# A two-attention, two-FFN sandwich on one core: one routing pass ahead of the scatters, and ScalarE applying the norms around the second attention's first tiles

## The reference

```python
x = x + LN(attn0(LN(x)))   # 16 heads of 64; x is 2 x 1024 x 128, float32
x = x + LN(ffn0(LN(x)))    # shared MLP, plus 8 experts with top-2 routing
x = x + LN(attn1(LN(x)))   # differential attention, 8 heads of 2 x 128
x = x + LN(ffn1(LN(x)))    # gated MLP with two hidden layers

def ffn0(h):
    n = h * rsqrt(mean(h*h) + 1e-8) * norm_weight
    shared = relu(n @ sw1 + sb1) @ sw2 + sb2
    probs = sigmoid(n @ router_w.T)              # 8 experts
    scores, idx = top_k(probs, 2)
    w = scores / (sum(scores) + 1e-6)
    return shared + sum_k w[k] * expert[idx[k]](n)
```

## Time and profile before

| | |
|---|---|
| three runs | 1982.66, 1984.46, 1985.24 us; median 1984.46 |
| profiled execution | 1987.63 us, with a span of 1985.6 us between the first and last instruction |
| busy in the span | PE 1826.1, DVE 1556.2, ACT 1354.5, POOL 1196.3 us |
| granted TensorE clock, mean | 0.972 of full |

### The profile page before, as it was taken

The page is one execution under the profiler, slowest core; times in us unless marked ns, Lnnn a source line. Parts: engine busy times, 40 slices in busy tenths (PEclk is TensorE's granted clock), DMA queues, the critical chain, the costliest instruction groups (busy, mean ns, idle before and its releaser), DMA issues.

```text
span 1985.6 us, 36444 instructions
## 1 busy us (share of the span) xinstructions
PE 1826.1 (92%) x11162; PEld 1557.8 (78%) x11162; DVE 1556.2 (78%) x2682; ACT 1354.5 (68%) x2739; POOL 1196.3 (60%) x1473
## 2 busy tenths in 40 slices
PE   4969999999999999976886899999999999999787
PEld 3858888878888888865775688888888888888666
DVE  5958999989989998964477877777777777777774
ACT  3848888878888887832454577777777777777555
POOL 4535655554656555653554677777777777777621
PEclk9989999999999999987998899999999999999899
DMA  2292121212121213021210000000000000100000
GB/s 71 47 86 50 45 48 45 50 46 48 45 50 45 48 45 94 22 86 55 67 57 30 4 1 12 1 11 0 11 0 11 0 11 0 66 1 1 1 11 11
DMA packets 68531, 65.95 MB, mean 33 GB/s; under 512 B 27712, under 2 KB 47040, under 8 KB 68128
## 3 DMA queue, kind: packets, MB, share of 16 engines
q1 hardware_dynamic: 65888, 59.02, 13.3%
q0 software_dynamic: 2496, 5.15, 0.7%
HBM read 21.33 MB, written 9.25 MB: 15 GB/s over the span
## 4 chain that ended last, share of the span: by engine, by line
PE 77%; DVE 9%; issue 5%; ACT 4%; SPq 2%; POOL 2%; DMA 1%; another core or an unknown queue 1%; DVEq 0%; ACTq 0%; POOLq 0%
PE ps_t L625 7%; PE ps_o L635 6%; PE ps_s L657 5%; PE ps_s L658 5%; PE ps_o L636 5%; PE ps_s L1831 5%; PE ps_s L1829 5%; PE ps_s L1830 5%; PE ps_t L1887 3%; PE ps_o L1903 3%; PE ps_o L1905 3%; PE ps_o L1904 3%; PE ps_t L1323 2%; DVE a_negmax L2033 1%; PE ps_m L614 1%
## 5 line engine op out<-in xcount | busy, mean ns | idle before, releaser
L807 DVE TENSOR_REDUCE a_negmax<-ps_s 128x1 f32<-128x1024 f32 x256 | 313.3, 1224 | 70.7 <-PE ps_s L658 57.2
L2033 DVE TENSOR_REDUCE a_negmax<-ps_s 128x1 f32<-128x1024 f32 x256 | 312.5, 1221 | 67.5 <-PE ps_s L1831 64.8
L738 ACT ACTIVATE a_pth<-ps_t 128x512 fp32r<-128x512 f32 x512 | 279.4, 603 | 115.4 <-PE ps_t L625 115.3
L1961 ACT ACTIVATE a_p<-ps_s,a_negmax 128x1024 f32<-128x1024 f32 x256 | 286.8, 1120 | 95.6 <-DVE a_negmax L2033 94.6
L793 DVE TENSOR_TENSOR a_ptl<-ps_t,a_pth 128x512 fp32r<-128x512 f32 x512 | 327.8, 682 | 6.5 <-ACT a_pth L738 6.2
L873 POOL TENSOR_TENSOR a_rsum<-a_sum,minus_one 128x1 f32<-128x1 f32 x256 | 141.1, 551 | 312.7 <-ACT a_p L768 310.1
L877 POOL TENSOR_SCALAR a_p<-a_p,a_rsum 128x1024 f32<-128x1024 f32 x256 | 289.8, 1132 | 53.4 <-POOL a_rsum L873 53.4
L2131 POOL TENSOR_TENSOR a_p<-a_p 128x1024 f32<-128x1024 f32 x128 | 307.5, 2402 | 10.7
L768 ACT ACTIVATE a_p<-ps_s,a_negmax 128x1024 f32<-128x1024 f32 x256 | 289.2, 1130 | 13.8 <-DVE a_negmax L807 13.8
L657 PE MATMUL ps_s<-a_kh,a_q 128*128 128x512 f32 x512 | 202.8, 396 | 30.5 <-DMA a_kh<-a_kh 26.9
L635 PE MATMUL ps_o<-a_pth,a_v 128*128 128x512 f32 x512 | 220.8, 431 | 7.2 <-DVE a_ptl L793 4.5
(11 more groups left out here) (299 smaller groups left out, 4155.7 us busy)
## 6 DMA issues: line engine op xcount, KB each, us to landing
a_q<-a_kh SPq DMA_DIRECT2D x64, 128.0 KB, 2.2
a_q<-a_kl SPq DMA_DIRECT2D x64, 128.0 KB, 2.4
a_kh<-a_kh SPq DMA_DIRECT2D x64, 128.0 KB, 2.2
a_kl<-a_kl SPq DMA_DIRECT2D x64, 128.0 KB, 2.3
a_w_raw<-in_l_w SPq DMA_DIRECT2D x8, 384.0 KB
f_xs_rows<-f_zero SPq DMA_DIRECT2D x4, 736.0 KB, 17.3
f_raw<-in_ffn_w SPq DMA_DIRECT2D x2, 1408.0 KB, 8.1
f_xs<-f_xs_rows SPq DMA_DIRECT2D x2, 1235.0 KB, 7.3
```

Of the source, the lines that this page charges most:

```text
L807: dve.tensor_reduce(a0_negmax[:, s % 4:s % 4 + 1], ps_s[:, s % 2, :, :], AX.XY, ALU.max, negate=True)\
L2033: dve.tensor_reduce(a1_negmax[:, s % 2, m:m + 1], ps_s[:, m, :, :], AX.XY, ALU.max, negate=True)\
```

## The change

It has two parts.

Part one, the head of the first FFN. The low parts of the FFN's first weights move from POOL to DVE (`f0_pool_w1_lo` becomes `f0_dve_w1_lo`, one ahead of the routing, four and four between `shared` steps). All four chunks are normed, turned and given logits first; then one routing pass handles all 16 tiles (`f0_dve_route(dve)`, operands twice as long), one `f0_pe_prefix` both groups, and only `f0_dve_place` stays per group. PE's shared MLP comes behind all logits. `f0_left` and `f0_tmp2` are gone; `f0_taken` and `f0_sum` have a group dimension. Chunk 3 turns through a bank of `ps_s`. On DVE the last `pt_lo` of the attention comes ahead of a norm.

Part two, the norms around the second attention's first tiles, chunks 0 to 3. `x1_apply` moves from DVE to ACT as an activation with a scale and a bias; POOL's `norm_factors` also makes that bias, -mean x rstd. The sum into X stays on DVE (`x1_sum`). In the first head the table becomes `X1_DVE`: both halves of the combination come a slot or more earlier, and chunk 3's norm ends in slot 5 and not in slot 7. POOL's factors stand ahead of its scaling and summing in slots 2 to 5, and the keys of chunks 2 and 3 come in slots 5 and 7 instead of 6 and 9.

```diff
@@ a0_dve, after the last slot
             pt_lo(g - 2, SLOTS - 2)
-            y0_norm(dve, 4, 0)
-            pt_lo(g - 1, SLOTS - 1)
             dve.wait_ge(S["a0_out_added"], n - 2)
             y0_norm(dve, 0, 1)
-            add_out(n - 2, 2)
+            pt_lo(g - 1, SLOTS - 1)
+            y0_norm(dve, 4, 0)
+            dve.wait_ge(S["a0_pv"], 4 * H0 - 1)
             for stage in range(1, 4):
                 y0_norm(dve, stage, 1)
-            f0_dve_turn(dve, 0)
+            add_out(n - 2, 2)
@@ f0_pe
-            up(0)
             f0_pe_turn(pe, 1)
             pe.wait_ge(S["a0_out_added"], 2 * H0)
             f0_pe_logits(pe, 0)
             f0_pe_logits(pe, 1)
-            down(0, lambda: route(0))
-            up(1)
-            down(1)
             f0_pe_turn(pe, 2)
-            up(2)
-            pe.wait_ge(S["f0_prefix_out"], 1)
             f0_pe_logits(pe, 2)
-            down(2)
             f0_pe_turn(pe, 3)
             f0_pe_logits(pe, 3)
-            up(3)
-            down(3, lambda: route(1))
+            up(0)
+            down(0, lambda: f0_pe_prefix(pe))
+            for c in range(1, NC):
+                up(c)
+                down(c)
@@ f0_dve
+            for stage in (1, 2, 3):
+                y0_norm(dve, stage, 2)
+            f0_dve_turn(dve, 0)
+            for stage in (1, 2, 3):
+                y0_norm(dve, stage, 3)
+            y0_norm(dve, 4, 2)
+            f0_dve_turn(dve, 1)
+            y0_norm(dve, 4, 3)
...
+            f0_dve_w1_lo(dve, 0)
+            f0_dve_route(dve)
             f0_dve_place(dve, 0)
...
+            f0_dve_turn(dve, 2)
+            f0_dve_turn(dve, 3)
             shared(0)
-            f0_dve_turn(dve, 2)
+            f0_dve_place(dve, 1)
+            for pos in range(1, 5):
+                f0_dve_w1_lo(dve, pos)
             shared(1)
-            y0_norm(dve, 4, 3)
-            f0_dve_turn(dve, 3)
+            for pos in range(5, NE):
+                f0_dve_w1_lo(dve, pos)
             shared(2)
-            f0_dve_route(dve, 1)
-            f0_dve_place(dve, 1)
-            expert = f0_read_words(dve)
-            shared(3)
             for g in range(NG):
                 f0_dve_weights(dve, g)
+            shared(3)
+            expert = f0_read_words(dve)
@@ norm_factors, new
+        def norm_factors(pool, n, par):
+            mean = mv[:, par, :, 0]
+            pool.wait_ge(S["norm_var"], n + 1)
...
+            pool.tensor_scalar(mean, mean, -1.0, 0.0, ALU.mult, ALU.add)
+            pool_rsqrt(pool, rstd[:, par, :], mv[:, par, :, 1], EPS_LN).then_inc(S["pool_step"], 1)
+            pool.wait_ge(S["pool_step"], pool_steps.next())
+            pool.tensor_tensor(mean, mean, rstd[:, par, :], ALU.mult).then_inc(S["norm_rstd"], 1)
@@ x1_apply, x1_sum
-        def x1_apply(dve, c, i):
+        def x1_apply(act, c, i):
+            par = x1_par(c, i)
+            act.wait_ge(S["norm_rstd"], NORM_F0 + 2 * c + i + 1)
+            act.wait_ge(S["x1_summed"], from0(c - 1 + i))
+            for k in range(TPC):
+                t = c * TPC + k
+                ins = act.activation(tile(Y, t) if i else tile(xhat, k), tile(X if i else Y, t), ACT.Identity,
+                                     scale=rstd[:, par, k:k + 1], bias=mv[:, par, k, 0:1])
+            ins.then_inc(S["x1_ready" if i else "x1_applied"], 1)
+        def x1_sum(dve, c):
+            dve.wait_ge(S["x1_applied"], c + 1)
+            xc = X[:, c * TPC:(c + 1) * TPC, :]
+            dve.tensor_tensor(xc, xc, xhat[:, :, :], ALU.add).then_inc(S["x1_summed"], 1)
@@ the first head's slots
-        X1_SLOTS = {1: ((x1_combine, 2, 0), (x1_combine, 2, 1)), 2: ((x1_stats, 2, 0),), 3: ((x1_apply, 2, 0), (x1_stats, 2, 1)),
-                    4: ((x1_apply, 2, 1), (x1_combine, 3, 0), (x1_combine, 3, 1)), 5: ((x1_stats, 3, 0),),
-                    6: ((x1_apply, 3, 0), (x1_stats, 3, 1)), 7: ((x1_apply, 3, 1),)}
+        X1_DVE = {1: (("combine", 2, 0), ("combine", 2, 1)), 2: (("stats", 2, 0), ("combine", 3, 0)),
+                  3: (("sum", 2), ("stats", 2, 1)), 4: (("combine", 3, 1), ("stats", 3, 0)), 5: (("sum", 3), ("stats", 3, 1))}
+        X1_FACTORS = {2: (2, 0), 3: (2, 1), 4: (3, 0), 5: (3, 1)}
```

More of the change, by code:

```diff
@@ L173, in sandwich_kernel @@
         f0_to = sb("f0_to", [P, NB])
-        f0_taken = sb("f0_taken", [P, GT + 3, NR])
-        f0_sum = [sb(f"f0_sum{i}", [P, GT + 5, NR]) for i in range(2)]
+        f0_taken = sb("f0_taken", [P, NG, GT + 3, NR])
+        f0_sum = [sb(f"f0_sum{i}", [P, NG, GT + 5, NR]) for i in range(2)]
         f0_rows = sb("f0_rows", [P, GT + 1, NR])
@@ new lines, in f0_dve_route @@
+            first, second = (f0_one[:, k, :, :].rearrange("p (g t) e -> p g t e", g=NG) for k in range(2))
+            a, b = f0_sum
+            step(dve.tensor_tensor(f0_taken[:, :, 2:GT + 2, :], first, second, ALU.add))
+            step(dve.tensor_tensor(a[:, :, 4:, :], f0_taken[:, :, 1:GT + 2, :], f0_taken[:, :, 0:GT + 1, :], ALU.add))
+            step(dve.tensor_tensor(b[:, :, 4:, :], a[:, :, 4:, :], a[:, :, 2:GT + 3, :], ALU.add))
+            dve.tensor_tensor(a[:, :, 4:, :], b[:, :, 4:, :], b[:, :, 0:GT + 1, :], ALU.add)\
@@ L1386, in block_relu @@
                 ins.then_inc(S["f0_b_relued"], 1)
-            f0_act_turn(act, 1)
-            f0_act_probs(act, 0)
-            relu(0)
-            relu(1)
-            f0_act_turn(act, 2)
-            relu(2)
-            f0_act_turn(act, 3)
-            f0_act_probs(act, 1)
-            relu(3)
+            for c in range(1, NC):
+                f0_act_turn(act, c)
+            f0_act_probs(act)
+            for c in range(NC):
+                relu(c)
             expert = f0_read_words(act)
@@ L1719, in a1_act_prepare @@
                 a1_act_q(act, i + 1, (0, *Q_PIECES[i]), ps_m[:, :])
+            if n in A1_APPLY:
+                x1_apply(act, *A1_APPLY[n])
         def a1_dve_prepare(dve, n):
@@ L2019, in slot @@
                     softmax(g, s, 1)
+                if first and s in X1_FACTORS:
+                    x1_apply(act, *X1_FACTORS[s])
                 if last and SLOTS - 4 <= s < SLOTS + 2:
@@ L2091, in slot @@
                     negmax(g, s, 0)
-                    if first and s in X1_SLOTS:
-                        for work, c, i in X1_SLOTS[s]:
-                            work(dve, c, i)
+                    if first and s in X1_DVE:
+                        x1_dve(dve, s)
                     spare_lo(h, s, first, last)
@@ L2149, in slot @@
                     rms(h, s)
+                if first and s in X1_FACTORS:
+                    c, i = X1_FACTORS[s]
+                    norm_factors(pool, NORM_F0 + 2 * c + i, x1_par(c, i))
                 if s == M_SLOT and not first:
```

140 lines of the change are left out of this document (54 added, 86 removed).

## The result

| | before | changed |
|---|---|---|
| runs | 1982.66 to 1985.84 us, median 1984.85 | 1970.04 to 1970.78 us, median 1970.49 |
| ratio of the two | | 0.9929, 95% interval 0.9917 to 0.9942 |
| profiled execution, span | 1987.63, 1985.6 us | 1970.77, 1968.2 us |
| granted TensorE clock, mean | 0.972 | 0.976 |

A forecast was written before the change was run, and what follows sets the result against it. Only PE's waits at the attention's end, first FFN's head and second attention's first head could give time; head 2, loop 1, first head 14 make 17 us: 1967.5 from the median, own range 1961 to 1975, 8-in-10 range 1949 to 1980.

The forecast's parts named there:

- head, with the hold: First FFN's head: if signals are held behind the scatters, first block at 922.4 against 923.97; 2 us gained.
- block loop: FFN block loop: four norm applications leave DVE for ACT, which is not the busiest; 1 us gained, -1 to 3.
- first head: Second attention's first head: PE's waits for chunks 2 and 3 shrink; 14 us gained, bounds 8 to 16.
- The range's own lower terms: Lowest gains in the forecast's own range: head 0, loop -1, first head 8 us; given as 1975.
- The hold recurs: First FFN's head: the run of 16 scatters holds `relu(2)` until 901.9, 1.8 us behind its end; first block 922.4.
- Rival, no hold: First FFN's head: PE ends the shared MLP inside the scatter run; head gains 16.5, total 31.5 us, 1953; chance 0.30.
- The three waits: First head: PE's waits of 9.72, 4.62 and 4.37 us fall by 5.2, 4.6 and 4.4, in all 14.2.
- the sum `L1800`: First head: DVE's sum of two SBUF inputs may be blocked beside POOL; takes 0.69 or 3.1 us.
- Rival, slower: First head, slots 2 to 5: POOL's factors ahead of scaling and summing delay PE, 4.5 us a slot; 1990; chance 0.06.

The follow-up runs named there:

- p1_head: The kernel before with only the first part of the diff (the first FFN's head), norms as before; ratio to before 0.9994 (0.9983 to 1.0005).
- second and third group: Follow-up kernels timed beside the kernel before on chips 11 and 8; the kernel before took 1964.7 and 1968.0 us there.
- l_late: The changed kernel with ACT's norms in the block loop, their sums and second statistics one block later; 1946.8 us (one run).
- h_pace: The changed kernel with a small POOL power operation behind each pair of the first group's scatters; 1967.26 us (one run).

## Why the prediction was right, and where it was not

The time, 1970.49, lies in the range and 3 us from the forecast 1967.5. The terms did less well than their sum, so part of that closeness is luck: the head gave more in the profile, the loop and the first head less.

| term | forecast | measured |
|---|---|---|
| head, with the hold | 2 | 6.7 in the profile, 4.0 in that of `p1_head`, 1.2 (-1.0 to 3.4) by the runs of `p1_head` |
| block loop | 1 | -2.0 in the profile; 0.4 where nothing is held |
| first head | 14 | 11.1, and 11.9 without the hold |

The range's own lower terms (0, -1 and 8) add to 7 us, which is 1977.5 and not the 1975 given; the outcome does not hang on it.

**The hold recurs.** Right, in place, and in its end (2.2 us behind the last scatter, 1.8 forecast). Wrong in what it catches: forecast was that `relu(2)` stops dead; it was stretched by 0.7 to 1.4 us a piece, and the stop came one chunk later. With `relu(2)` done, only `relu(3)` and `down(3)` stood behind the release: 12.1 us from there to the first block, where the forecast had 20.5. The release itself came 3.0 us later (904.90, not 901.9), so the first block is 5.4 us earlier than forecast, and with a low clock in `down(3)` (6.58 us in `p1_head`) 2.7 of it go again.

**Rival, no hold.** Its mechanism was seen in full in the second and third group, at a first block of 909.09 where the forecast said 907.5. Its gain of 16.5 us in the head was not: the kernel before loses its hold as well (A + B 84.5), and the difference is 8.0. The forecast compared the changed kernel without a hold to the old one with it.

**Loop.** The step said that ACT's four norms lie in its slack, with a gain of 1. The term is mis-sized: without the hold the gain is 0.4. ACT's time did lie in its slack (1.65 us each, 1.15 by the nearest row), but its wait did not: the order of ACT's list puts `block_relu` behind a wait for POOL's factors, and the prediction did not name what is queued behind that wait. That this ate what DVE's relief gave is likely and not shown; `l_late`, with the wait gone, takes 5 us out of the loop. With the hold the loop lost 2.0, 1.5 of them ahead of ACT's first norm; why is not known.

**First head.** The three waits were foreseen as 14.2 us less. Those for the turns fell by 6.5 and 4.2, as forecast 5.2 and 4.4; the third fell by 3.0 of 4.6. New waits of 0.98 (for POOL's `a_p`) and 1.25 us came in, both from POOL's lateness. The Trainium skill ("SBUF — State Buffer", section "SBUF: two separate sides") has VectorE's operations with two SBUF inputs shut out beside GpSimd operations that read SBUF. The trace agrees: where I had looked for it, at the sum `L1800`, it cost 1.1 us once; where I had not, at a one-column `a_c` with two SBUF inputs, it cost 2.1 us twice.

**Rival, slower.** Its mechanism, factors ahead of scaling and summing, is real: 4.7 us over four slots, 1.2 a slot, where 3.5 would have turned the sign.

What stays open: by which way a run of indirect DMAs holds PE's signals, and why in one group and not in the others. Each group ran on another chip and at another time, and no kernel was timed on two chips in one group or on one chip in two, so the chip and the moment can't be told apart.

## What to carry to other kernels

Work that moves to an engine with slack brings its waits with it: look at what is queued behind the wait, and place the work one step after its input is sure to be there; here that was worth 5 us, while taking the work off DVE had gained 0.4 in that stretch. Do the same for the producer: a small reciprocal root ahead of a long pass on POOL made every later tile late. And a gain that rests on a stall should be priced against a kernel before that may not have the stall either.

## What was not expected of the hardware

An unbroken run of POOL's indirect DMAs (of 5 to 16, one every 1.27 us) delayed PE's signals to ACT and DVE, first by 0.7 to 1.4 us each and then until about 2 us behind the run. A pause of 1.1 us behind every second one took the delay away in `h_pace` (one run). In the second and third group, on other chips, runs of 16 and of 26 such DMAs delayed nothing, in the same two kernels too; the 20 us between 1985 and 1965 us lie in the stretches where the delays were.

A VectorE operation on one column per partition took 2.32 us beside POOL's sum of maps (128x1024, 2.38 us), and 0.22 alone: what is shut out pays by the other's length, not by its own.
